# Gate logits from the turned attention output with multiplied-out weights, expert choice on the logits, output projection behind the dispatch

## The reference

```python
x = x + attention(cond_ffn(x, cond_8), ...)          # 16 heads; scores pass a 3-tap convolution over the keys
# attention ends with: out @ Wo.T + bo
y = x @ W_base.T + b_base + lora                     # per batch entry: y = x @ Weff[b] + b_base
gates = softmax(y @ wg); expert_idx = argmax(gates)  # 8 experts, 128 slots each
locations = cumsum(one_hot(expert_idx)) - 1          # slot within the expert
disp[slot] += y                                      # dispatch
h = relu(disp @ w1 + b1); eo = h @ w2 + b2           # per expert
out = x + eo[slot] * gate_val                        # combine, weighted by the largest gate
```

## Time and profile before

| | us |
|---|---|
| median of 3 runs | 263.09 (262.97 to 263.28) |
| profiled execution, whole | 265.03 |
| profiled execution, span from first to last instruction | 263.1 |
| PE busy | 239.2 (91%) |
| DVE busy | 209.1 (79%) |
| ACT busy | 168.5 (64%) |
| POOL busy | 143.0 (54%) |

### The profile page before, as it was taken

How to read it: one execution, slowest core, us unless ns; L and a number is a source line. 1 busy time by engine, 2 the same in 40 slices (tenths; PEclk the granted TensorE clock), 3 DMA queues, 4 the chain that set the end, 5 groups by cost and what they waited for, 6 DMA issues and landing times.

```text
span 263.1 us, 5532 instructions
## 1 busy us (share of the span) xinstructions
PE 239.2 (91%) x1775; PEld 186.7 (71%) x1775; DVE 209.1 (79%) x509; ACT 168.5 (64%) x307; POOL 143.0 (54%) x166
## 2 busy tenths in 40 slices
PE   7996978989898998999999879799998999999993
PEld 7454856867676776867877757578777876879982
DVE  1549899888979889897987998979979666677553
ACT  2643589967778687787868557778679660214321
POOL 1019779978679787787968446779783000000000
PEclk9999879999999999999999999999999999999998
DMA  6950007456273535637353507163544704400002
GB/s 206 360 232 0 0 4 220 144 120 189 51 226 133 120 122 118 198 99 182 125 120 123 118 31 210 59 183 123 120 165 120 196 4 125 197 0 2 0 2 80
DMA packets 13766, 31.73 MB, mean 121 GB/s; under 512 B 1458, under 2 KB 10674, under 8 KB 13490
## 3 DMA queue, kind: packets, MB, share of 16 engines
q1 hardware_dynamic: 13314, 30.82, 38.9%
q10 hardware_dynamic: 432, 0.65, 0.8%
HBM read 19.14 MB, written 12.32 MB: 120 GB/s over the span
## 4 chain that ended last, share of the span: by engine, by line
PE 62%; DVE 14%; issue 9%; ACT 6%; POOL 4%; DMA 2%; DVEq 1%; SPq 0%; ACTq 0%; POOLq 0%
PE sc L829 8%; PE tp L974 8%; PE sc L831 6%; PE sc L830 6%; PE pvbank L850 6%; PE pvbank L848 5%; DVE Pb L554 5%; PE sc L1060 3%; PE tp L1070 3%; DVE w2s L689 2%; ACT Kh L354 2%; POOL Kl L256 2%; ACT Pb L359 2%; DVE kc L498 2%; PE sc L1020 1%
## 5 line engine op out<-in xcount | busy, mean ns | idle before, releaser
L359 ACT ACTIVATE Pb<-Pb,nbias 128x512 f32<-128x512 f32 x128 | 90.9, 719 | 42.2 <-DVE Pb L554 41.0
L554 DVE TENSOR_SCALAR_CACHE_REDUCE Pb<-sc,col 128x512 f32<-128x512 f32 x128 | 92.0, 738 | 15.1 <-PE sc L831 13.9
L829 PE MATMUL sc<-Kh,Ql 128*128 128x512 f32 x124 | 57.6, 465 | 9.0 <-issue 4.6
L256 POOL TENSOR_TENSOR Kl<-kc,Kh 128x512 fp32r<-128x512 f32 x29 | 37.5, 1292 | 31.0 <-ACT Kh L354 30.3
L974 PE MATMUL tp<-cst,Pb 128*128 128x128 f32 x332 | 50.3, 275 | 4.1 <-ACT PT L406 4.0
L974 PEld LDWEIGHTS tp<-cst,Pb 128*128 128x128 f32 x332 | 40.5, 141 | 17.4 <-issue 4.9
L831 PE MATMUL sc<-Kh,Qh 128*128 128x512 f32 x124 | 49.3, 398 | 0.0
L830 PE MATMUL sc<-Kl,Qh 128*128 128x512 f32 x124 | 49.3, 397 | 0.0
L406 ACT ACTIVATE PT<-tp 128x512 f32<-128x512 f32 x79 | 46.0, 582 | 1.2 <-PE tp L974 1.2
L268 POOL TENSOR_TENSOR td<-ta,tc_ 128x512 f32<-128x512 f32 x31 | 41.2, 1329 | 2.6
L261 POOL TENSOR_SCALAR ta<-Kp,cwS 128x512 f32<-128x512 f32 x31 | 30.5, 983 | 16.0 <-ACT Kp L332 15.9
(11 more groups left out here) (241 smaller groups left out, 305.7 us busy)
## 6 DMA issues: line engine op xcount, KB each, us to landing
swap<-w2s SPq DMA_DIRECT2D x15, 768.0 KB, 3.3
PT<-swap SPq DMA_DIRECT2D x60, 192.0 KB, 3.9
w1s<-in_w SPq DMA_DIRECT2D x1, 2048.0 KB, 10.6
w2s<-in_w SPq DMA_DIRECT2D x1, 2048.0 KB, 7.9
cst<-in_consts SPq DMA_DIRECT2D x1, 648.0 KB, 6.2
xTs<-in_xT SPq DMA_DIRECT2D x2, 256.0 KB, 3.5
we<-in_wexp SPq DMA_DIRECT2D x2, 256.0 KB, 4.0
b2s<-in_b2row SPq DMA_DIRECT2D x1, 512.0 KB, 11.4
```

What stands on the lines that cost most here:

```text
L256: pool.tensor_tensor(Kl[:, n, :], kc[:, n, :], Kh[:, n, :].bitcast(f32), ALU.subtract)\
L359: act.activation(Pb[:, k, :], Pb[:, k, :], ACT.Exp, bias=nbias[:, k:k + 1], scale=-1.0)\
L554: dve.tensor_scalar(Pb[:, k, :], SC[k % 4][:, :], cb, None, ALU.subtract, ALU.min, accum_out=nbias[:, k:k + 1]).then_inc(s["mx"], 1)
L829: pe.matmul(SC[k][:, :], ql, Kh[:, h2, :], start=True, stop=False)
```

## The change

The logits are no longer computed from z but from OT and xTs with weights that carry the gate's wg already: weffg = Weff wg, wzg = Wo Weff wg, bzg = the bias times wg. They are made in the first units of attention (*weights*, three parts on PE and DVE); step 12 goes. Step 3 compares the logits with their maximum; the exponentials are used for the gate value alone, in a new step 13. Steps 2 and 3 change places in entry 0. For entry 1 PE's order is written anew, with step 1 behind most of the dispatch and steps 7 and 4 between the first experts' up and down; the keep_busy matmuls go. ACT's high_half runs one unit earlier, at u%4 = 3, with the first one ahead of unit 0.

```diff
-AT_PE = {(0, 5): 12, (0, 10): 0, (0, 12): 2, (0, 14): 3, (1, 1): 6, (1, 3): 1, (1, 6): 7, (NG - 1, 10): 4,
-         (NG - 1, 13): 5}
-AT_ACT = {(0, 11): 0, (0, 13): 2, (0, 15): 3, (1, 7): 7, (NG - 1, 11): 4, (NG - 1, 14): 5}
-AT_DVE = {(0, 6): 12, (0, 15): 3, (1, 2): 6, (1, 4): 1, (1, 5): 7, (1, 9): 8, (NG - 1, 10): 9, (NG - 1, 12): 10,
+AT_PE = {(0, 10): 0, (0, 12): 3, (0, 14): 2, (1, 1): 6, (1, 3): 1, (1, 6): 7, (NG - 1, 10): 4, (NG - 1, 13): 5}
+AT_ACT = {(0, 11): 0, (0, 14): 3, (0, 15): 2, (1, 7): 7, (NG - 1, 11): 4, (NG - 1, 14): 5}
+AT_DVE = {(0, 13): 3, (1, 2): 6, (1, 4): 1, (1, 5): 7, (1, 6): 13, (1, 9): 8, (NG - 1, 10): 9, (NG - 1, 12): 10,
...
-                if u % QT == 0 and (not isinstance(g, int) or hd + 2 < B * H):
-                    high_half(hd + 2, (u // QT) % 2)
+                if u % QT == 3 and (not isinstance(g, int) or hd + 3 < B * H):
+                    high_half(hd + 3, (u // QT + 1) % 2)
...
+            high_half(2, 0)
...
-            for k in (0, 2, 3, 4, 5):
+            for k in (0, 2, 3, 5):
...
+            hidden(0)
             after(1, 7)
-            hidden(0)
+            after(1, 4)
...
-                    dve.tensor_tensor(lg[:, :, :], L, over_experts(lmax), ALU.subtract).then_inc(s["nl"], 1)
-                    dve.wait_ge(s["nla"], b + 1)
-                    dve.tensor_reduce(gmax, es[:, :, :], AX.X, ALU.max).then_inc(s["gm"], 1)
-                    step(dve.tensor_reduce(ssum, es[:, :, :], AX.X, ALU.add))
-                    step(dve.reciprocal(rs, ssum))
-                    dve.tensor_tensor(es[:, :, :], es[:, :, :], over_experts(rs), ALU.mult).then_inc(s["gm"], 1)
-                    dve.wait_ge(s["gm"], 3 * b + 1)
-                    dve.tensor_tensor(gmax, gmax, rs, ALU.mult).then_inc(s["gm"], 1)
-                    dve.wait_ge(s["gm"], 3 * b + 3)
-                    step(dve.tensor_tensor(eq[:, :, :], es[:, :, :], over_experts(gmax), ALU.is_equal))
+                    step(dve.tensor_tensor(eq[:, :, :], L, over_experts(lmax), ALU.is_equal))
                     step(dve.scalar_tensor_tensor(eq[:, :, :], eq[:, :, :], -float(E), io8, ALU.mult, ALU.add))
                     step(dve.tensor_reduce(idx, eq[:, :, :], AX.X, ALU.min))
                     dve.scalar_tensor_tensor(mask[:, tiles, :], io8, -float(E), over_experts(idx),
                                              ALU.add, ALU.is_equal).then_inc(s["msk"], 1)
+                    dve.tensor_tensor(lg[:, :, :], L, over_experts(lmax), ALU.subtract).then_inc(s["nl"], 1)
...
+                elif k == 13:
+                    dve.wait_ge(s["nla"], b + 1)
+                    step(dve.tensor_reduce(ssum, es[:, :, :], AX.X, ALU.add))
+                    step(dve.reciprocal(gmax, ssum))
...
+            def weights(k):
+                at = MISC[:, B * C + B:B * C + B + B * E].rearrange("p (b e) -> p b e", e=E)
+                if k == 0:
+                    dve.wait_ge(s["wfm"], 1)
+                    dve.tensor_copy(weffT[:, :, :], MISC[:, 0:B * C].rearrange("p (b m) -> p b m", b=B))\
+                        .then_inc(s["wft"], 1)
+                elif k == 1:
+                    dve.wait_ge(s["wgm"], 1)
+                    dve.tensor_copy(wz[:, :, :], MISC[:, 0:B * C].rearrange("p (b m) -> p b m", b=B))\
+                        .then_inc(s["wze"], 1)
+                    dve.tensor_scalar(bz[:, :], MISC[:, B * C:B * C + B], col[:, BB:BB + 1], None, ALU.add)\
+                        .then_inc(s["wze"], 1)
+                    dve.tensor_copy(weffg, at).then_inc(s["wge"], 1)
+                    dve.wait_ge(s["wze"], 2)
+                    for b in range(B):
+                        dve.tensor_scalar(bzg[:, b, :], col[:, WG:WG + E], bz[:, b:b + 1], None, ALU.mult)\
+                            .then_inc(s["wge"], 1)
+                else:
+                    dve.wait_ge(s["wpm"], 1)
+                    dve.tensor_copy(wzg, at).then_inc(s["wpe"], 1)
...
+                if u in (6, 8):
+                    weights(u // 2 - 3)
                 unit(0, 0, u)
+            weights(2)
...
-            for k in (1, 3, 5, 6, 8, 9, 10, 11, 7):
+            for k in (3, 6, 8, 5, 9, 10, 11):
+                after(1, k)
+            dve.wait_ge(s["dsp"], 2)
+            dve.tensor_copy(DT[:, 512:1024], SC[1][:, :]).then_inc(s["dted"], 1)
+            for k in (1, 7, 13):
                 after(1, k)
             spread(6, 0)
             spread(7, 0)
-            dve.wait_ge(s["dsp"], 2)
-            dve.tensor_copy(DT[:, 512:1024], SC[1][:, :]).then_inc(s["dted"], 1)
             dve.wait_ge(s["b2"], 16)
...
+            def gate_inputs(b):
+                bank = STAGE_BANK[b][3]
+                if b == 0:
+                    pe.wait_ge(s["on"], 2 * NG + 1)
+                    pe.wait_ge(s["wge"], B + 1)
+                    pe.wait_ge(s["wpe"], 1)
+                pe.matmul(bank[:, 0:QT * E].rearrange("p (t e) -> p t e", e=E), ones[:, :],
+                          bzg[:, b:b + 1, :].broadcast_to([128, QT, E]), start=True, stop=False)
+                for q in range(QT):
+                    pe.matmul(bank[:, q * E:(q + 1) * E], xTs[:, S * b + q * 128:S * b + (q + 1) * 128],
+                              weffg[:, b, :], start=False, stop=False)
+            def earlier_tiles(at):
+                for p in range(QT):
+                    pe.matmul(at, ones_r[:, :], mask[:, p:p + 1, :].broadcast_to([128, QT, E]),
+                              start=(p == 0), stop=False)
+            def weights(k):
+                at = MISC[:, B * C + B:B * C + B + B * E].rearrange("p (b e) -> p b e", e=E)
+                if k == 0:
+                    pe.wait_ge(s["vev"], B)
+                    for i in range(B):
+                        mm = pe.transpose(MISC[:, i * C:(i + 1) * C], weff[:, i, :], ident)
+                    mm.then_inc(s["wfm"], 1)
+                elif k == 1:
+                    pe.wait_ge(s["wft"], 1)
+                    for i in range(B):
+                        pe.matmul(MISC[:, i * C:(i + 1) * C], wq[:, 4, :], weff[:, i, :], start=True, stop=True)
+                        pe.matmul(MISC[:, B * C + i:B * C + i + 1], weff[:, i, :], col[:, BO:BO + 1],
+                                  start=True, stop=True)
+                        mm = pe.matmul(at[:, i, :], weffT[:, i, :], col[:, WG:WG + E], start=True, stop=True)
+                    mm.then_inc(s["wgm"], 1)
+                else:
+                    pe.wait_ge(s["wge"], B + 1)
+                    for i in range(B):
+                        mm = pe.matmul(at[:, i, :], wq[:, 4, :], weffg[:, i, :], start=True, stop=True)
+                    mm.then_inc(s["wpm"], 1)
...
                 elif k == 1:
-                    if b == 0:
-                        pe.wait_ge(s["slt"], 1)
+                    pe.wait_ge(s["slt"] if b == 0 else s["nl"], b + 1)
                     pe.wait_ge(s["ote"], b + 1)
...
+                        pe.wait_ge(s["nl"], 1)
...
-                    pe.wait_ge(s["zte"], b + 1)
+                    pe.wait_ge(s["ote"], b + 1)
+                    if b == 0:
+                        gate_inputs(b)
                     for q in range(QT):
-                        mm = pe.matmul(bank[:, q * E:(q + 1) * E], zT[:, q * 128:(q + 1) * 128],
-                                       col[:, WG:WG + E], start=True, stop=True)
+                        mm = pe.matmul(bank[:, q * E:(q + 1) * E], OT[:, q * 128:(q + 1) * 128], wzg[:, b, :],
+                                       start=False, stop=(q == QT - 1))
                     mm.then_inc(s["lgm"], 1)
...
+                if u in (5, 7, 9):
+                    weights((u - 5) // 2)
...
-                pe.matmul(SC[h][:, :], Zl[:, t, :], D[:, t, 512 * h:512 * (h + 1)], start=(t == 0), stop=False)
-                mm = pe.matmul(SC[h][:, :], Zh[:, t, :], D[:, t, 512 * h:512 * (h + 1)],
+                pe.wait_ge(s["zhi"], t // QT + 1)
+                pe.matmul(SC[h][:, :], Zh[:, t, :], D[:, t, 512 * h:512 * (h + 1)], start=(t == 0), stop=False)
+                pe.wait_ge(s["zlo"], t // QT + 1)
+                mm = pe.matmul(SC[h][:, :], Zl[:, t, :], D[:, t, 512 * h:512 * (h + 1)],
...
             last_outputs(1)
+            gate_inputs(1)
             pe.wait_ge(s["on"], 2 * B * NG - 1)
             for i in range(QT):
                 pe.wait_ge(s["raw"], B * NG + (1 if i < QT - 1 else 2))
                 mm = pe.transpose(MISC[:, i * 128:(i + 1) * 128], RAW[:, i * 128:(i + 1) * 128], ident)
             mm.then_inc(s["otr"], 1)
+            project_x(1)
+            after(1, 0)
             dispatch(1, 0)
+            after(1, 3)
+            after(1, 2)
             dispatch(1, 1)
-            after(1, 0)
-            project_x(1)
-            for k in (2, 1, 3, 4, 5):
-                after(1, k)
+            after(1, 6)
             dispatch(2, 0)
+            after(1, 5)
             dispatch(2, 1)
-            keep_busy(TP[0], 4)
-            after(1, 6)
```

(22 more changed lines are left out.)

31 lines of the change are left out of this document (16 added, 15 removed).

## The result

| | before | after |
|---|---|---|
| median of the runs, us | 263.18 (262.97 to 263.51, 4 runs) | 272.68 (271.08 to 273.80, 4 runs) |
| profiled execution, whole / span, us | 265.03 / 263.1 | 273.61 / 271.7 |
| mean granted clock of PE in it | 0.983 | 0.973 |
| ratio after to before | | 1.0333 (95%: 1.0291 to 1.0375) |

The change makes the kernel 9.5 us slower. The forecast was 266.7 us, with 261.5 to 269.3 as its range: the sign was right, the size was not. The four runs of after had mean clocks of 0.973, 0.973, 0.978 and 0.984. That row, which a reader passes over easily, turned out to be the answer.

What follows compares the result with a forecast made beforehand. The prediction took a loop through DVE, ACT and PE to set each pair of heads (10.99 us). First units +3.8, Kh +0.6, stage of entry 0 −0.5 and end −0.3 made +3.6: 263.1 to 266.7 us, range 261.5 to 269.3.

Steps and rivals of the forecast that it cites:

- half speed in part of it: First units, after PE's wait for V: the granted clock drops, so unit 10's scores come 0.9 us later.
- First units: Start of attention, where DVE has no gap: Kh moved ahead and three weights parts add 3.8 us (2.3 to 5.0).
- (b): First units, weights part 0: PE waits for V with unit 10's scores queued behind; +0.8 us.
- (c): First units, weights part 1: twelve PE instructions hold unit 12's scores, then DVE has the copy and four small operations; +2.1 us.
- (a): First units: Kh of head 2 ahead of unit 0 moves POOL's td onto the middle tap, which ends later; +0.8 us.
- Kh one unit earlier: Every head: ACT's idle is won, but POOL's td catches the middle tap; +0.6 us in sum (−6.7 to +3).
- worth nothing: Pairs of heads: removing the second tap's collision (1.39 us) gains nothing, since DVE waits for PE afterwards anyway.
- Stage of entry 0: Pairs around entry 0's gate: step 12 gone −0.75, gate's pair +1.2, next pair −1.0; together −0.5 us (−1.8 to +1.2).
- End: After attention: dispatch ends 1.1 us sooner, but work moved behind it costs 0.8; −0.3 us (−1.2 to +0.8).
- A: Rival: POOL's wait was the bound, PE's waits for Kl come back as gain up to 6.7 us; 260.4; chance 0.17.
- B: Rival: half speed through part 1 (5.0) and td over the tap in both kinds of pair (+3); 270.3; chance 0.11.
- C: Rival: gains and losses cancel, with part 1's wait hidden, ACT's gaps filled and no collision; 262.6; chance 0.12.

Runs made afterwards that it cites:

- m1: The changed kernel plus eight matmuls at 22.5 us, six ahead of part 0's wait for V, and the gate's row parted in two: 266.33 us.
- m2: The kernel before plus eight wide matmuls in PE's gap at 22.5 us: 263.33 us, 12 of 12 runs at full clock.
- the repeat: The changed kernel run again unaltered, beside the variants on one chip: 269.36 us, 1 of 6 runs at full clock.
- e2: The kernel before with only Kh made one unit earlier: 264.74 us, ratio 1.0010 to before.
- f3: The kernel before with the change's end and choice on logits alone; step 12 kept, Kh late, no weights in advance: 263.12 us.
- e1: The changed kernel with Kh put back to units 0, 4, 8 and 12: 266.84 us, lowest 265.25.
- e3: The changed kernel with all three parts of the weights moved from the first units into entry 1's first group: 267.76 us.
- h4: The kernel before with the change's end and Kh one unit earlier, no precomputed weights: 262.80 us, 9 of 12 runs at full clock.
- h3: The kernel before with the change's end, and PE waiting for V after unit 5 with no weights computed: 265.31 us.
- k3: The kernel before with the change's end, and 18 calls (36 instructions) of narrow 128x8 matmuls in entry 1's third pair: 269.34 us.
- f2: The changed kernel with Kh late again and all weights moved to entry 1's first group: 266.53 us, 0 of 9 at full clock.
- e4: The changed kernel with weights moved to entry 1's first group except part 0, left in the first units: 267.54 us (265.05 to 271.18).

## Why the prediction was right or wrong

**At full clock the sum came near, by luck.** +3.6 forecast, +3.0 measured between m1 and m2; 266.7 forecast, 266.33 in m1 and 266.58 in the one run of the repeat at full clock. But its four terms were +3.8, +0.6, −0.5 and −0.3, and came out at about +2.7, −0.6, +1.5 and −0.6, as worked out below: three errors of 1 to 2 us, which cancel.

**The step that failed** is the cost of the clock, "half speed in part of it". The text names 0.9 us for it, takes up some 0.25 (the +0.8 of part 0 less 0.35 of work and 0.2 of waiting), and puts it at nothing anywhere else: behind the gate there was no term for it, and none for the stretch that the base had. Its price was some 6 us: 6.4 between the medians of the changed kernel and m1, 3.0 between those of its repeat and m1. The changed kernel's profiled execution has three stretches. The one at 25 to 29 puts the minimum of unit 5 at 33.30, against 31.39 in m1: 1.9. From there to the first pair it takes 24.5 against 21.2: 3.3, with the stretch from 39 to 45 in it. The gate's pair takes 16.66 against 15.0 without: 1.65. Together 6.9 of the 7.5 us between the spans of the changed kernel and m1. Not all of the 3.3 is the stretch: the repeat's profile, with a stretch at 38 to 41, no caught tap there and a wait for V of 2.2 instead of 4.28, takes 23.3 from the minimum of unit 5 to the first pair, 2.1 over m1.

**The base was mixed.** The text set the median equal to the span, because both read 263.1. The execution that the profile shows took 265.03; it has half clock at 25 to 29 us. The windows and the minimum of unit 5, before and then m2:

```profile
26.00:28.00 2.00, 2.00 (x6) 0.50 0.00 0
33.49 0.73 DVE L554 TENSOR_SCALAR_CACHE_REDUCE Pb<-sc,col 128x512 f32<-128x512 f32 x1
...
26.00:28.00 2.00, 2.00 (x11) 1.00 0.00 0
31.57 0.74 DVE L554 TENSOR_SCALAR_CACHE_REDUCE Pb<-sc,col 128x512 f32<-128x512 f32 x1
```

The runs of the median, 1.9 shorter, most likely did not have that (they were not profiled). The base was right by luck: time and span differ by 1.9 us, and so do the runs with that stretch and those without. The earlier trace rows gave the clock of 30 to 40 us as 0.83 and was read as the price of a wait; it belonged to a second stretch at 35 to 39, which cost nothing (33.49 to 52.08 is 18.6 us, 18.8 in m2).

**First units, +3.8:** +2.2 at full clock (52.59 against 50.37), and 0.5 more in the first two pairs (23.2 against 22.7 in e2), where m1 has a caught tap (57.00, 1.57) that is free in e2. Of it (b) is 0.7 (0.8 forecast: the minimum behind the copy at 38.77 against 38.23, V 0.2 sooner) and (c) 1.4 (2.1: unit 12's minimum 2.09 behind unit 11's, against 0.70). (a), the collision of td and the middle tap, is there in the changed kernel's profile as forecast (1.52 instead of 0.75) and absent at full clock: in m1 the tap starts at 33.35 and td at 35.48. The place of POOL against DVE had been read from an execution in which half clock had held DVE back by 2 us. Where a tap is caught it ends 0.56 us after td (both rows of after), near the 0.55 of the rows and not the 0.71 of a whole tap.

**Kh one unit earlier, +0.6:** −0.6 (e2 against f3: 0.2 ahead of the first pair, 0.4 in the pairs). The mechanism was right: the first tap of every second pair is caught (1.50 to 1.58 in e2), and three such pairs are 0.45 to 0.7 longer, against 0.36 forecast. The failing step here is the one that called the removal of the second tap's collision "worth nothing": the two pairs behind the gate's shrink from 14.55 to 13.71 and from 12.39 to 12.00, the first from 11.03 to 10.69. In the changed kernel the part was no gain (265.25 with Kh late, e1, against 266.58, one run of each at full clock); that is the next term.

**Stage of entry 0, −0.5:** +1.5 (the gate's pair and the second behind it, e3 against e2; with the gate parted, m1 has about 0.5 less). The gate's pair was right (+1.1 for 1.2, from 13.93 to 15.0). Step 12's −0.75 was right where Kh is late (11.76 to 10.89 in e1) and 0 where Kh is early (11.56 with it in e2, 11.58 without): it seems that behind the longer loop its work had become free. The terms were added as if independent. The −1.0 in the next pair was Kh's, not the gate's: 13.71 in e2 and in the whole change alike. The second pair behind the gate's is 0.5 longer (12.00 to 12.47). h4 has that too, and with Kh late there is none of it (12.39 in f3, as before): likely the sum of the exponentials (step 13), again only with Kh early; it was not priced.

**End, −0.3:** −0.6 (56.33 against 56.93).

**The rivals.** A (POOL's wait) is refuted by e2: most of the waits go, and the time stays. (Its sum, 263.1 + 3.8 − 6.7 − 0.8, is 259.4 and not 260.4; nothing else rests on it.) B, at 270.3, named half speed through part 1 and two collisions; the first was there, larger than priced, the second not as a loss. C's cancelling did not come. The Trainium skill, "TensorE: Matmul & The Clock Gate", section "What's actually happening", says that the unit's idle state is the throttled one and activity releases it. The prediction held it against the wait for V alone, at +4.7 for the first part, and took "only a part of it". h3 agrees with the page: 2.24 us of standing, and 11 of 12 runs are not at full clock. But the section speaks of activity without saying what kind, and k3 shows a PE that works without a gap and falls.

**What stays open.** Why of one kernel some runs have a given stretch and others not is not explained. f2 does the same as the kernel before up to 120 us, and its profile has the stretch at 25 to 28; yet 0 of its 9 runs were at full clock against 49 of 97. Nor was it tried whether the gate's row by itself, at its own length and in a kernel otherwise at full clock, brings half clock.

## What to carry to other kernels

Read the granted clock of each run before any other row, of the base too, and make the base of a sum an execution at full clock. A step that makes the matmul unit wait for a result two microseconds away, or that strings together many narrow matmuls, can cost by the clock besides its work: the wait alone cost 0.3 us at full clock (263.27 against 262.93, one run against nine) and 2.2 in the median; wide matmuls into a free bank are cheap where the unit stands anyway (eight of them here: the lowest time 0.3 us up, 12 of 12 runs at full clock). And terms of one loop don't add: where one edit lengthens it, another's gain is already hidden.

## What the hardware showed that was not expected

Half clock appears in and behind a row of narrow matmuls although PE's busy share reads 1.00: 0 of 6 runs at full clock with 36 instructions of 128x8 (4.1 us), 5 of 7 with 32 of 128x128 (3.7 us). The price of one instruction rose from 0.113 us (4.08 for 36) to 0.167 (10.68 for 64) over the row in which the clock fell. Runs of one kernel differ by whole stretches: 265.05 and 271.18 us in e4, at clocks of 0.998 and 0.977, with nothing else on record between them.
